# Node pass of a four-layer graph kernel: where three norms' sums are kept, how z3 is made, and the order of the work

## The reference, cut to what matters

```python
h0 = x @ W1b + b1;               x1 = ln(x + relu(ln(h0) * g + b) @ W2 + b2)
h1 = x1 @ W + bias;              x2 = ln(x1 + gelu(ln(h1) * gamma + beta))
xl = elu(x2 @ Wl1 + bl1 + bias1) @ Wl2 + bl2        # 64 wide, also stored
z3 = elu(xl + bias2);            z4 = elu(z3 @ Wlin + blin)
x3 = ln(x2 + z4);                x4 = ln(x3)
```

## Time and profile before

| what | value |
| --- | --- |
| time, median of 3 runs | 4524.6 us (4520.72 to 4529.36) |
| span of the profiled execution (the page gives no other time for it) | 4555.5 us |
| PE busy over the span | 3736.2 us, 82% |
| DVE busy | 3567.4 us, 78% |
| ACT busy | 3254.0 us, 71% |
| POOL busy | 2447.4 us, 54% |
| node pass: fill ("in") | 65.4 to 133.6 us |
| node pass: 13 turns of the loop | 133.6 to 1313.8 us |
| node pass: drain ("out") | 1313.8 to 1387.1 us |

### The profile page before, as it was taken

How to read it: one execution, slowest core, us unless ns; L and a number is a source line. 1 busy time by engine, 2 the same in 40 slices (tenths; PEclk the granted TensorE clock), 3 DMA queues, 4 the chain that set the end, 5 groups by cost and what they waited for, 6 DMA issues and landing times. The chain is left out here.

```text
span 4555.5 us, 74285 instructions
## 1 busy us (share of the span) xinstructions
PE 3736.2 (82%) x19896; PEld 2525.2 (55%) x20115; DVE 3567.4 (78%) x5989; ACT 3254.0 (71%) x10835; POOL 2447.4 (54%) x2740
## 2 busy tenths in 40 slices
PE   3999999999986999996888868888867776777675
PEld 2777777777763666664555544555434443444444
DVE  3777777777775878885888868999979996667776
ACT  2999999999994888884999974555557775333333
POOL 3666666666646777753343314333155552667775
PEclk9999999999997999998999989999989998888888
DMA  2455544554543333322333323333234443222321
GB/s 52 126 133 135 132 128 133 134 132 127 134 117 96 87 93 85 92 67 74 85 89 85 86 57 93 106 107 107 75 103 117 122 117 93 76 79 80 85 81 44
DMA packets 690753, 451.53 MB, mean 99 GB/s; under 512 B 138595, under 2 KB 618185, under 8 KB 690624
## 3 DMA queue, kind: packets, MB, share of 16 engines
q1 hardware_dynamic: 504736, 310.80, 25.2%
q0 software_dynamic: 56528, 81.64, 7.2%
q10 hardware_dynamic: 129360, 57.82, 4.6%
HBM read 252.90 MB, written 199.90 MB: 99 GB/s over the span
## 5 line engine op out<-in xcount | busy, mean ns | idle before, releaser
L224 ACT ACTIVATE node_z<-psum 128x128 f32<-128x128 f32 x1960 | 508.8, 287 | 30.4 <-PE psum L204 29.1
L1162 POOL DMA_INDIRECT slot_src_rows<-x,slot_index x392 | 425.4, 1085 | 172.7 <-issue 109.9
L609 ACT ACT_TABLE_LOAD x397 | 509.4, 1283 | 7.6 <-ACT slot_new L1279 0.4
L224 ACT ACTIVATION_READ_ACCUMULATOR node_z<-psum 128x1 f32 x1960 | 430.5, 220 | 0.0
L224 ACT ACTIVATE slot_logit<-psum 128x128 f32<-128x128 f32 x980 | 256.4, 280 | 174.3 <-PE psum L204 170.1
L204 PE MATMUL psum<-center,slot_t 128*128 128x128 f32 x1176 | 216.3, 287 | 92.6 <-ACT slot_t L218 50.0
L850 DVE TENSOR_TENSOR node_x<-psum,node_rstd 128x512 f32<-128x512 f32 x294 | 200.9, 683 | 111.6 <-POOL node_rstd L945 109.8
L1553 DVE TENSOR_TENSOR_SCAN slot_den<-slot_expo,slot_den 128x512 f32<-128x512 f32 x147 | 188.2, 1280 | 116.0 <-ACT slot_expo L218 91.3
L942 POOL TENSOR_TENSOR node_variance<-node_mean_square,eps 128x4 f32<-128x4 f32 x196 | 80.5, 411 | 362.3 <-ACT node_z L224 355.8
L1162 POOL DMA_INDIRECT slot2b_src_rows<-xl,slot2b_index x196 | 225.4, 1150 | 83.5 <-issue 48.9
L1148 POOL DMA_INDIRECT out_nodes<-slot_new,slot_side_index x196 | 219.8, 1121 | 91.7 <-POOL slot_side_index L1142 43.9
(11 more groups left out here) (400 smaller groups left out, 12659.0 us busy)
## 6 DMA issues: line engine op xcount, KB each, us to landing
x<-node_x SPq DMA_DIRECT2D x294, 256.0 KB, 3.0
slot_keep<-keep SPq DMA_DIRECT2D x147, 256.0 KB
node_xT<-in_x_T SPq DMA_DIRECT2D x98, 256.0 KB
out_nodes<-node_x SPq DMA_DIRECT2D x98, 256.0 KB
x<-slot_new ACTq DMA_DIRECT2D x98, 256.0 KB
slot_dst_rows<-x SPq DMA_DIRECT2D x98, 256.0 KB
staged<-node_gathered SPq DMA_DIRECT2D x98, 128.0 KB, 2.5
xl<-node_xl SPq DMA_DIRECT2D x98, 128.0 KB, 3.4
```

The source lines that it names most:

```text
L224: ins = act.activation(g.z[u][:, t, :], rows[:, t, :], ACT.Square, scale=float(D ** -0.5), accum_out=g.mean_square[u][:, t:t + 1])
L609: act.add_instruction(mybir.InstLoadActFuncSet(name=nc.get_next_instruction_name(), ins=[], outs=[], act_func_set_id=wanted[0]))
L1162: pool.indirect_dma_start(src_rows[u][:, t, 0:src_width], None, table, at_index(index[u][:, t:t + 1], 0))\
```

## The change

Three things are edited in the node pass, and its table of starts is another one.

1. The sums of squares of `sq0`, `sq2` and `sq4` are written to the unused bank 7 of PSUM instead of a small SBUF tile, and the Ln reads them there. `sq1` and `sq3`, which GpSimd reads, stay in SBUF.
2. `z3` is no longer a product: the rows of `xl`, which ScalarE has copied to SBUF, are turned by TensorE, four tiles of 128 x 64, the first as a product with the identity and three as transposes. They hold the bias `bl2` already, so `exp3` and `h3` use `bias2` alone.
3. `z4` multiplies by `Wlin_full`, 128 rows of which the last 64 are zero, and reads all 128 rows of `act_T`.
4. `PLAN["node"]` has other numbers, in another unit (the period is 73.538 in place of 12.80); only their order matters. The rewritten `order_of_work` gives the same order for a table without delays, as all are.

```diff
-        "node": (12.80, (4.154, 2.724, 12.612, 15.996, 16.388, 14.741, 14.897, 22.597, 22.836, 30.776, 36.936,
+        "node": (73.538, (2.229, 13.254, 19.588, 38.780, 56.064, 18.722, 102.108, 93.524, 108.044, 138.059, 40.603, 57.489,
...
-def act_squares(act, g, u, rows):
+def act_squares(act, g, u, rows, sums):
 
     for t in range(TILES):
         ins = act.activation(g.z[u][:, t, :], rows[:, t, :], ACT.Square, scale=float(D ** -0.5),
-                             accum_out=g.mean_square[u][:, t:t + 1])
+                             accum_out=sums[u][:, t:t + 1])
...
+    c.Wlin_full = sb("Wlin_full", [P, D])
...
+        sums = [c.psum[:, NODE_STREAMS, u * TILES:(u + 1) * TILES] for u in g.streams]
...
-                    act_squares(act, g, u, tiles_of(A(u)))
+                    act_squares(act, g, u, tiles_of(A(u)), sums if step in ("sq0", "sq2", "sq4") else g.mean_square)
...
-                    act_copy(act, g, u, g.variance[u][:, :], g.mean_square[u][:, :], ACT.Ln, c.eps[:, 0:1])
+                    act_copy(act, g, u, g.variance[u][:, :], sums[u], ACT.Ln, c.eps[:, 0:1])
...
-                    act_copy(act, g, u, expz[u][0:C2, :], A(u)[0:C2, :], ACT.Exp, c.node_bias2[:, 0:1])
+                    act_copy(act, g, u, expz[u][0:C2, :], A(u)[0:C2, :], ACT.Exp, c.bias2[:, 0:1])
...
                     pe.wait_ge(*g.ACT.done(u, i, "xl"))
-                    pe.matmul(A(u)[0:C2, :], c.Wl2[:, :], act_T[u][:, :], start=True, stop=True).then_inc(g.pe_out[u], 1)
+                    pe.matmul(A(u)[0:C2, tile_cols(0)], xl[u][:, 0, :], c.ident[:, :], start=True, stop=True)
+                    for t in range(1, TILES):
+                        ins = pe.transpose(A(u)[0:C2, tile_cols(t)], xl[u][:, t, :], c.ident[:, :])
+                    ins.then_inc(g.pe_out[u], 1)
...
-                    pe.matmul(A(u), c.Wlin[:, :], act_T[u][0:C2, :], start=True, stop=True).then_inc(g.pe_out[u], 1)
+                    pe.matmul(A(u), c.Wlin_full[:, :], act_T[u][:, :], start=True, stop=True).then_inc(g.pe_out[u], 1)
```

More of the change, by code:

```diff
@@ L119, with order_of_work @@
 }
-def order_of_work(chain, phase, streams, others=()):
-    period, starts, between = PLAN[phase]
+def order_of_work(chain, phase, streams):
+    period, starts, delays = PLAN[phase]
     placed = []
     for u in range(streams):
+        delay = delays[u] if delays else 0.0
         for (engine, step), start in zip(chain, starts, strict=True):
-            now = start + u * period
+            if delays and step == "gelu1":
+                delay += delays[streams + u]
+            if delays and step.startswith(("gather", "put", "store_staged")):
+                delay = 0.0
+            now = start + u * period + delay
             placed.append((now % (streams * period), u, int(now // (streams * period)), engine, step))
-    for n, step in enumerate(others):
-        placed.append((n // len(between) * period + between[n % len(between)], -1, 0, "POOL", step))
     placed.sort(key=lambda item: item[0])
@@ L167, in every_turn, with plan @@
     run(SLOT_ITERS, "out")
-def plan(g, chain, phase, others=()):
-    g.order = order_of_work(chain, phase, len(g.streams), others)
+def plan(g, chain, phase):
+    g.order = order_of_work(chain, phase, len(g.streams))
     for steps, engine in ((g.PE, "PE"), (g.ACT, "ACT"), (g.DVE, "DVE"), (g.POOL, "POOL")):
@@ L429, in _ @@
                              (all_ones, 1.0), (c.minus_one_col, -1.0), (c.self_src, 0.0), (c.pair_src, 0.0),
-                             (c.value_bias2, 1.0)):
+                             (c.value_bias2, 1.0), (c.Wlin_full, 0.0)):
                 pool.memset(t[:, :], value).then_inc(made, 1)
-            pool.wait_ge(made, 21)
+            pool.wait_ge(made, 22)
             pool.affine_select(out=c.ident[:, :], in_=c.ident[:, :], compare_op=ALU.not_equal, fill=1.0, base=0,
@@ L440, in _ @@
                                    pattern=[[-(D // h), h], [0, D // h]], channel_multiplier=1).then_inc(made, 1)
-            pool.wait_ge(made, 26)
+            pool.wait_ge(made, 27)
             for h, t in same_head.items():
@@ L444, in _ @@
                                    pattern=[[D // h, h], [0, D // h]], channel_multiplier=-1).then_inc(made, 1)
-            pool.wait_ge(made, 29)
+            pool.wait_ge(made, 30)
             pool.wait_ge(map_started, 16)
@@ L453, in _ @@
                 v.tensor_tensor(keep[o][:, :], row_here[o][:, :], row_prev[o][:, :], ALU.is_equal).then_inc(masks, 1)
-            v.wait_ge(made, 29)
+            v.wait_ge(made, 30)
             v.tensor_scalar(c.center[:, :], c.ident[:, :], -1.0 / D, None, ALU.add).then_inc(worked, 1)
@@ L468, in _ @@
             for out, source in ((c.Wl2r2[:, 0:C2], c.Wl2[:, :]), (c.Wl2r2[:, C2:], c.Wr2[:, :]),
[L469 removed]
+                                (c.Wlin1[0:C2, :], c.Wlin[:, :]), (c.Wlin_full[0:C2, :], c.Wlin[:, :]), (c.pair_src[0:C2, 0:C2], c.ident[0:C2, 0:C2]),
                                 (c.pair_dst[:, 0:C2], c.ident[:, C2:]),
@@ L479, in _ @@
             v.tensor_scalar(c.value_bias2[0:C2, :], c.bias2[:, :], 1.0, None, ALU.add).then_inc(worked, 1)
-            setup += 10
+            setup += 11
             to_center = ((raw["W1a"], c.W1a), (raw["W1b"], c.W1b), (raw["W2"], c.W2), (c.W, c.Wc),
@@ L572, in _ @@
             pe.wait_ge(loaded, 16 * len(loads))
-            pe.wait_ge(made, 29)
-            pe.wait_ge(worked, 24)
+            pe.wait_ge(made, 30)
+            pe.wait_ge(worked, 25)
             pe.matmul(psum[:, 6, 0:D], all_ones[:, :], c.Wl2r2[:, :], start=True, stop=True)
@@ L578, in _ @@
             pe.transpose(psum[:, 0, 0:D], c.W[:, :], c.ident[:, :]).then_inc(products, 1)
-            pe.wait_ge(worked, 24 + 7 + 13 + 3 + 8 + 5 * 8 + 1)
+            pe.wait_ge(worked, 25 + 7 + 13 + 3 + 8 + 5 * 8 + 1)
             for b, lhs, rhs, m in ((1, WT, S["att_src"], D), (2, WT, S["att_dst"], D), (3, raw["Wn"], S["a_src"], D),
@@ L894, in work @@
                 elif step == "h3":
-                    elu(u, i, C2, "h3_em1", c.node_bias2)
+                    elu(u, i, C2, "h3_em1", c.bias2)
                 elif step == "h4_em1":
@@ L1253, in work @@
                     act.wait_ge(*g.PE.done(u, i, squares[step]))
-                    act_squares(act, g, u, tiles_of(A(u)))
+                    act_squares(act, g, u, tiles_of(A(u)), g.mean_square)
                 elif what == "log":
```

1 line of the change is left out of this document (removed), and 10 rows, old and new, of the table PLAN.

## The result

The changed kernel takes 4503.4 us (4500.13 to 4505.93, 5 runs) against 4524.6: a ratio of 0.9954, 95% interval 0.9942 to 0.9967. That is 21 us faster, inside the range, with somewhat over half of the 38.7 us that the prediction summed. The profiled execution has a span of 4498.4 us.

A forecast was written before the change was run, and what follows sets the result against it. ScalarE was taken to bound the kernel at 12.73 us a chunk, a TensorE-VectorE chain afterwards at 12.25; 91 x 0.48 = 43.7 us less, 5 more from the drain: 4524.6 - 38.7 = 4486 us, range 4443 to 4514.

The forecast's parts named there:

- VectorE's part of the chain: From x2T's start through its copy, h3_em1 and h3 to z4: 2.49 us of the chain expected to rule.
- The chain that I expect to rule: Node pass, once a period: x2T, VectorE's copy, h3, z4, then TensorE's queue to the next x2T; taken as 12.25 us.
- The chain is longer: Rival, chance 0.13: chain longer or accumulator reads into PSUM slower, 12.5 to 12.6 us a period, 4513 us.
- Sums in PSUM: ScalarE's queue per chunk: 0.13 us less for three Ln reading PSUM, 0.25 less for twelve accumulator reads writing there.
- ScalarE by new order: ScalarE's queue per chunk: the new places of the Ln save 0.64 us, from 12.73 to 12.09.
- I take that as even: ScalarE's 14 table loads a turn, now behind squares and gelu1, were taken to cost the same as before.
- `z3`: TensorE: replacing the 1.00 us product by five instructions of 0.12 saves 0.4 us a chunk (0.35 to 0.7).
- `z4` stays: TensorE: z4 with 128 weight rows costs as much as with 64, whose instruction has 641 ns.
- Drain +5: End of node pass: transfers behind each rstd5 add 5 us, bounds 0 and 10.
- In fill and drain I count no gain: Start and end of the node pass, outside the loop's steady turns: no time saved there was counted.

The follow-up runs named there:

- e1: The changed kernel with SP's stores of x3 and xl behind the load of the next stream instead of ahead of it: 4473.4 us, ratio 0.9880.
- e2: The changed kernel with the sums of sq0, sq2 and sq4 back in SBUF: 4515.1 us, ratio 0.9974 to the kernel before.
- e4: The changed kernel's parts 1 to 3 with the table of starts of the kernel before: 4509.8 us, ratio 0.9965.
- e12: The kernel before with the new table of starts alone, none of the other three parts: 4541.3 us, ratio 1.0037.
- e6: e1 with every ScalarE step 0.665 of a period later, same order, so the loop turns ahead of an Ln: 4467.2 us, ratio 0.9868.
- e3: The changed kernel with z3 again the product with Wl2, in its new place: 4528.6 us, ratio 0.9998 to the kernel before.
- e11: The changed kernel with z4's weights laid out as before, 64 rows: 4517.4 us, ratio 0.9982 to the kernel before.
- e5: e1 with h3_em1 and h3 ahead of the copy of x2T on VectorE and z4 ahead of z2 on TensorE: 4477.2 us, ratio 0.9892.
- e9: e1 with y2 ahead of z3 on TensorE and the squares of sq4 ahead of exp3 on ScalarE: 4468.6 us, ratio 0.9875.

## Why the prediction came out as it did

**Right.** Faster, and inside the range. ScalarE's queue got shorter than TensorE's needs, ScalarE now waits for `y2`, and the weight load of `z4` waits for `h3`. VectorE's part of the chain is 2.49 us, to the hundredth. The undisturbed chunk, 12.15 us, lies near the forecast 12.25 and within its 12.1 to 12.4.

**The step that failed: the move of SP's load.** "The chain that I expect to rule" weighs what stands beside VectorE's part, but no step of the prediction asks where the load of `node_xT` stands in SP's queue, though SP's queue was moved with the others. It went behind two stores, its lead fell from 7.0 to 4.3 us against a landing of 3.9, and the mean chunk came to 12.49. e1 undoes only this and gains 30 to 33 us, more than the 18 us that were missing. With 12.49 the time is that of the rival "The chain is longer" (12.5 to 12.6, 4513 us), though the reason is neither of the two that the rival names.

**Terms that were mis-sized.**
- "Sums in PSUM": 0.25 us for the twelve reads are 0.13, since the reads themselves come 0.04 later; 0.13 for the three Ln are 0.07 (0.05 for one, 0.02 for the two that stand together). The two together are 0.20 by e2's timeline and its chunk and 0.23 by e4, not 0.38. The sign was right; the Trainium skill's remark that the write's half overlaps with the next instruction (Perfetto Trace Analysis, Optimizing Scalar/DVE Operations) is nearer than its rule of 93 against 51 ns taken for every instruction: the trace gives 12 ns for each read and square.
- "ScalarE by new order": as a length of ScalarE's queue the 0.64 us was right. In e1 two waits are hidden from start to start, 0.18 us ahead of `sq4` (441.81 to 442.56, where 0.57 is what `exp3` costs) and 0.11 ahead of `sq1` (440.49 to 440.80 against 0.20), so the queue is 12.15 - 0.29 = 11.86 us. The sums account for 0.20 of the 0.87 saved and the order for the other 0.67. In the time it is not seen: the order brought e12 a chunk of 12.74 in place of 12.73, because TensorE was then the longer queue. It pays only together with parts 2 and 3, which shorten TensorE. "I take that as even" holds for the table loads inside a chunk: one behind squares starts 0.41 us behind the last square (608.66 to 609.07 in the changed kernel) where ordinary work starts 0.25 behind, one behind an Exp 0.22 (1289.65 to 1289.87 before) in place of 0.10. It missed the turn of the loop, which costs ScalarE 3.0 us in place of 1.85, as a table load now stands first in it. 13 x 1.15 = 15 us were at stake; e6 puts an Ln there and gets back 5 to 6.
- "`z3`": 0.28 us less rather than 0.4 (0.72 against 1.00). e3 gives 20 us for it: it is the largest of the three parts.
- "`z4` stays": wrong. The duration of an instruction was compared, 641 ns, where the distance to the next start was wanted. It stood in the trace of before, where `z4` takes 1.05 to 1.11 us to the next start, mostly 1.05 or 1.06, and `z2` 0.96. The row shown has the upper value:

```profile
600.73 1.12 PE L829 MATMUL psum<-node_act_T,Wlin 64*128 64x512 f32 x2
601.84 0.66 PE L213 MATMUL psum<-ident,node_x 128*128 128x128 f32 x4
```

  e11 gives 13 us for the part.
- "Drain +5": the distance behind the last `rstd5` grew by 7.0 us, to 12.0, beyond the 7 to 10 forecast: the landing with the change of phase took 6.4 us and not 2.2 to 4.3 above the issues. "In fill and drain I count no gain" missed the fill: with the store of gathered rows moved behind it, the first load left 6.6 us earlier, and the first square came 6.9 us earlier. Both ends together gave 9.7 us (20.4 less 10.7). With 6.9 gained at the start and 7.0 lost at the end, another 10 us must have been gained in the fill or the drain; where is not shown.

Adding up the misses: the loop gained 10.7 us for 43.7, 33 us less than forecast; the ends gained 9.7 for a loss of 5, 15 us more. The 33 are 91 x (12.49 - 12.25) = 22 for the late load and 13 x (2.5 - 1.7) = 11 for the dearer turn (89.96 - 7 x 12.49 against 90.78 - 7 x 12.73), which the sum had held at its old price. The two errors half cancel in the time, and that is luck: with the ends as forecast, 10.7 less 5, the kernel would have taken 4519 us, outside the range that ends at 4514.

**What rules at 12.15.** A ring is a chain of waits that comes back to its own start one chunk later; the longest one sets the period. Two are nearly equally long here, and the prediction had one of them. The other goes through ScalarE: `xl`, `z3`, `y2`, the squares of `sq4` and on to the next `xl`. In e5, where the predicted chain is cut, both of its waits are seen in nearly every chunk (`z3` for `xl`, the squares for `y2`), and the chunk is 12.15. In e1 the ring is there as well, though the list of waits has little of it: ScalarE loses 0.18 us ahead of `sq4`, and the weight load of `z3` waits for `xl` 81 times (23.3 us). e9 opens this ring, its waits show no such row, and the chunk goes to 12.08, not to the 11.96 that I then expected. There ScalarE's queue is 11.83 and TensorE's at most 11.6 without its waits for VectorE's copy ahead of `z2` and for `h3` ahead of `z4`. That is the predicted chain, at 12.08 in place of 12.25.

The other chunks fit this. e2 makes only ScalarE's work longer, by 0.20, and its chunk is 12.15 + 0.20 = 12.35. e11 makes only `z4` longer, which stands in the predicted chain and not in the ring, by 0.10, and its chunk is 12.08 + 0.10 = 12.18. That 12.08 is the predicted chain is argued from waits and from these sums. A kernel with e9's order and both waits for VectorE taken out, which would test it, was not tried.

## What to carry to other kernels

When a new order is read, every queue it touches is to be walked, the one that only starts transfers too: for each load, its lead (issue to first use) is to be set against its landing time, because one late load every other chunk undid more than half of the gain. An instruction is to be priced by the distance to the next start, not by its own duration. And an order and the edits under it are not additive: the order alone cost 17 us and the edits alone gained 18, while with the order in place the three parts are worth 9, 20 and 13 us.

## What the runs showed of the hardware

- A float32 product with 64 weight rows costs 0.10 us more until the next start than one with 128 (1.06 against 0.96 us, two instructions of 512 columns), though both have durations of 641 to 645 ns. In the old order it is 1.05 or 1.06 (before) against 0.92 (e4) in most chunks. e11 measured 13 us for 98 chunks. Why is not shown.
- An ACTIVATION_READ_ACCUMULATOR into PSUM frees ScalarE 0.04 us sooner (0.05 against 0.09) and the next read comes 0.04 us later behind its ACTIVATE (0.20 against 0.16). Four pairs take 0.95 us in place of 1.00, ahead of a table load 1.13 in place of 1.16.
- A wait of up to 0.25 us can stand in a timeline without being listed as idle time: in e9 ScalarE's squares start 0.45 us behind two Exp that cost 0.20 without a wait.
- ScalarE's turn of a hardware loop costs 1.7 to 1.9 us ahead of an Ln and 2.6 to 3.0 ahead of a table load.
